# Transposed scores in the latent attention, a halved gate in the retention, and a new order of the first stage

## The chip, the cores and the metric

One Trainium2 chip, one of its cores. A core has five engines with queues of their own: TensorE (PE, matrix products into PSUM), VectorE (DVE), ScalarE (ACT), GpSimd (POOL) and SyncE (SP), which here issues the transfers. They meet through semaphores. The metric is the device time of one execution in microseconds (us).

## The reference

Six layers are applied to x (2 x 64 rows of 512), one after the other, each as x = x + layer(layernorm(x)): a latent cross-attention, an attention with sign-quantised weights, a mixture of 32 experts, a second cross-attention, a retention with group norm and gate, and a mixture of 128 mixed experts. The change touches the first and the fifth, and the sums of absolute weights of the second.

```
# first: latent cross-attention, 16 heads, 1024 context rows of 128
q_hk   = (layernorm(x) @ Wq.T).reshape(b, s, H, K)
q_big  = einsum('bshk,hkq->bshq', q_hk, w_kc_q)
kv     = kv_c * cos + rotate_half(kv_c) * sin           # rope
scores = einsum(q_big @ W_qr, kv @ W_kr)                # b h s l
ctx_c  = einsum('bhsl,bld->bhsd', softmax(scores), kv)
out    = einsum('bhsd,hkd->bshk', ctx_c, w_kc_kv).reshape(b, s, H*K) @ Wo.T
# fifth: retention
y   = ((q @ k.T) * 32**-0.5 * decay) @ v                # q, k rotated, 16 heads of 32
yn  = (y - mean) / sqrt(var + eps) * gn_weight + gn_bias
out = (silu(x @ w_g) * yn) @ w_proj
```

## The kernel before

All 128 rows of x stand on the 128 partitions. Each engine has one program, written out in order, and the order of the work is that of these programs.

**First stage.** The weights of the 16 heads come in four groups. SP issues, in this order: x, the constants (identity, mask and more), the query weights of group 0 in two halves, rank weights 0, wkr, query and rank weights 1, the same of 2, the context, the rope tables, query and rank weights 3, ctx64, then the 5 MB of wb. For a group g, `queries(g)` (L1077) makes the queries, `qrk_products(g)` (L1064) and `qkw_products(g)` (L1103) multiply the low-rank weights together, and `latent_queries(g)` (L1117) joins both; DVE's `at_copy`, `bw_copy` and `qk_copy` and ACT's copies bring each result from PSUM to SBUF. POOL makes the rotated half of rope (L405 to L411), DVE the other half and the sum (`rope`, L685); `context_transposes` (L1091) and ACT's `kvT_copy` turn the result. PE's order is L1179 to L1201.

**The loop of units.** A unit is two heads of one batch element, 128 rows; there are 16. Loop L1202 has in each pass the scores of unit i (`scores`, 128 rows on the partitions, 1024 keys in two PSUM banks), the result transpose of i-3, the context products of i-2 and the eight transposes of the probabilities of i-1. DVE takes the row maximum (L729) and ACT the exponential with the row sum (L480); both then copy half of the transposed probabilities (L736, L488); DVE scales the context by the reciprocal sum (L744). DVE also sums the absolute weights of the next layer (L763), and ACT takes their signs (L513). Behind it come `latent_values` and the output product (L1229).

**The retention.** PE makes projections 0 and 1 (q, k), the gate (`projection(3)`) and v (`projection(2)`), each eight instructions at L1508, then scores (L1533), y (L1541), the residual, and 18 products of ones (`keep_clock`, L1038) that compute nothing. DVE meanwhile makes weight x gate and bias x gate (L941 to L943), y x weight, the variance, its root on ACT, the division and the bias, in two halves of 256 columns (L951 to L966). PE transposes each half (`gated_transposes`) and multiplies by w_proj (L1563).

`link` makes DVE wait for its own last result.

## Time and profile before

| What | us |
|---|---|
| median of 3 runs (lowest, highest) | 358.01 (357.06, 358.23) |
| the profiled execution | 358.2 |
| its span, first to last instruction | 356.4 |
| PE busy | 346.5 (97%) |
| DVE, ACT, POOL busy | 146.4, 92.4, 39.3 |

The span is what the profile shows; 1.8 us of the time lie around it. PE's busy share counts every instruction from its start to its modelled end, so it says that PE is seldom without work, not that the work is all needed. The first stage runs from 8 to about 45.7 us, the loop of units to about 117, the retention from 281 to about 310.

### The profile page before, as it was taken

The numbers are of one execution on the slowest core, as the hardware profiler recorded it, in microseconds if no ns is written. First come the engines' busy times: TensorE is split into PE (matmuls) and PEld (weight loads), VectorE is DVE, ScalarE is ACT, GpSimd is POOL, SyncE is SP. The second block draws the span as 40 slices with busy tenths as digits, with TensorE's granted clock in tenths as the row PEclk, the third lists the DMA queues.
The fourth block names the chain that finished last, engine by engine and source line by source line (L and its number), as shares of the span: only waits on it lengthen the run. The fifth ranks groups of instructions, "written<-read, shape, count | busy, mean of one in ns | idle before, by whom it ended". The sixth has DMA issues, their size and how long they took to land.

```text
span 356.4 us, 5185 instructions
## 1 busy us (share of the span) xinstructions
PE 346.5 (97%) x2108; PEld 211.2 (59%) x2110; DVE 146.4 (41%) x318; ACT 92.4 (26%) x185; POOL 39.3 (11%) x77
## 2 busy tenths in 40 slices
PE   8898999999999999999999999999999999999997
PEld 6798677777778557555444443434366545554455
DVE  2118465777552134835213212321276245653131
ACT  1011344556543001423313121212112125030110
POOL 1006000000000002023000000000049300102110
PEclk9999999999999999999999999999999999999999
DMA  7999999920000700007598999899989910000000
GB/s 249 424 422 451 411 427 423 417 99 3 0 2 2 294 0 2 0 2 295 206 403 356 371 425 362 348 419 388 428 346 424 428 54 2 0 0 0 2 0 29
DMA packets 7800, 79.41 MB, mean 223 GB/s; under 512 B 993, under 2 KB 1761, under 8 KB 2913
## 3 DMA queue, kind: packets, MB, share of 16 engines
q1 hardware_dynamic: 7776, 79.09, 54.4%
q8 instruction: 17, 0.28, 0.3%
q14 instruction: 7, 0.05, 0.0%
HBM read 78.82 MB, written 0.26 MB: 222 GB/s over the span
## 4 chain that ended last, share of the span: by engine, by line
PE 85%; DMA 6%; DVE 3%; SPq 2%; ACT 1%; issue 1%; ACTq 0%
PE ps L1411 12%; PE ps L1577 10%; PE ps L1137 8%; PE ps L1160 8%; DMA ra<-in_wq 6%; PE ps L1439 5%; PE ps L1458 4%; PE ps L1229 4%; PE ps L1508 4%; PE ps L1149 4%; PE ps L1394 3%; PE ps L1450 2%; PE ps L1280 2%; PE ps L1372 2%; PE ps L1300 1%; PE ps L1598 1%
## 5 line engine op out<-in xcount | busy, mean ns | idle before, releaser
L1411 PE MATMUL ps<-rd,ra 128*64 128x384 f32 x256 | 44.4, 489 | 0.1
L1411 PEld LDWEIGHTS ps<-rd,ra 128*64 128x64 f32 x256 | 18.0, 137 | 26.5 <-issue 26.1
L1160 PEld LDWEIGHTS ps<-rd,ra 128*128 128x128 f32 x256 | 29.9, 192 | 4.4 <-issue 4.1
L1160 PE MATMUL ps<-rd,ra 128*128 128x128 f32 x256 | 31.3, 275 | 0.0
L1137 PE MATMUL ps<-rd 128*128 128x512 f32 x64 | 30.2, 594 | 0.0
L900 DVE SCALAR_TENSOR_TENSOR ra<-ra,ps 128x192 f32<-128x192 f32 x16 | 5.7, 354 | 59.3 <-ACT ra L584 59.3
L1577 PE MATMUL ps<-rd,xnT 128*128 128x512 f32 x64 | 28.0, 593 | 0.0
L480 ACT ACTIVATE ra<-ps,sv 128x1024 f32<-128x1024 f32 x16 | 17.8, 1116 | 35.0 <-DVE sv L729 35.0
L1038 PE MATMUL ps<-ones 128*128 128x256 bf16 x161 | 24.0, 296 | 1.0 <-POOL ones L390 1.0
L729 DVE TENSOR_REDUCE sv<-ps 128x1 f32<-128x1024 f32 x16 | 19.6, 1222 | 12.5 <-PE ps L1137 12.5
L584 ACT ACTIVATE ra<-ps 128x192 f32<-128x192 f32 x16 | 5.3, 331 | 65.9 <-PE ps L1411 65.9
L396 POOL TENSOR_SCALAR sv<-sv 128x1 f32<-128x1 f32 x6 | 1.5, 249 | 188.0 <-DVE sv L666 184.8
L1038 PEld LDWEIGHTS ps<-ones 128*128 128x128 bf16 x161 | 16.6, 107 | 7.2 <-issue 3.4
L1577 PEld LDWEIGHTS ps<-rd,xnT 128*128 128x128 f32 x64 | 11.9, 190 | 14.2 <-issue 14.2
L1439 PE MATMUL ps<-rd,ra 128*64 128x512 f32 x64 | 17.3, 618 | 0.0
L1087 PE MATMUL ps<-xnT,ra 128*128 128x128 f32 x128 | 15.3, 278 | 2.0 <-DMA ra<-in_wq 1.9
L1149 PE MATMUL ps<-cst,ra 128*128 128x128 f32 x128 | 16.6, 273 | 0.0
L1087 PEld LDWEIGHTS ps<-xnT,ra 128*128 128x128 f32 x128 | 14.6, 192 | 2.8 <-DMA ra<-in_wq 2.6
L1137 PEld LDWEIGHTS ps<-rd 128*128 128x128 f32 x64 | 10.9, 190 | 7.8 <-issue 7.6
L1149 PEld LDWEIGHTS ps<-cst,ra 128*128 128x128 f32 x128 | 14.5, 141 | 0.0
L1508 PE MATMUL ps<-rb,xnT 128*128 128x512 f32 x32 | 14.3, 593 | 0.0
L1229 PE MATMUL ps<-rb,ra 128*128 128x512 f32 x32 | 14.1, 595 | 0.0
(259 smaller groups left out, 487.4 us busy)
## 6 DMA issues: line engine op xcount, KB each, us to landing
rd<-in_ring SPq DMA_DIRECT2D x8, 2560.0 KB, 8.8
rd<-in_ring SPq DMA_DIRECT2D x8, 2048.0 KB, 8.5
rd<-in_f1gu SPq DMA_DIRECT2D x8, 1024.0 KB, 14.2
rb<-in_wb SPq DMA_DIRECT2D x1, 5120.0 KB, 34.9
ra<-in_e SPq DMA_DIRECT2D x2, 2560.0 KB, 17.1
rb<-in_b SPq DMA_DIRECT2D x1, 5120.0 KB, 21.2
ra<-in_wr SPq DMA_DIRECT2D x4, 1152.0 KB, 15.3
ra<-in_wq SPq DMA_DIRECT2D x3, 1024.0 KB, 14.8
```

Source lines behind the costliest of these rows:

```text
L480: act.activation(prob_x[u % 2].rearrange("p j l -> p (j l)"), ps[:, 2 * (u % 2):2 * (u % 2) + 2, :].rearrange("p a n -> p (a n)"), ACT.Exp ...
L729: dve.tensor_reduce(mx_x[:, u:u + 1], ps[:, 2 * (u % 2):2 * (u % 2) + 2, :].rearrange("p a n -> p (a n)"), AX.X, ALU.max, negate=True).the ...
L1038: pe.matmul(ps[:, bank, 0:256], idle[:, 0:P], idle, start=True, stop=True)
L1087: ins = pe.matmul(ps[:, g % 2, h * P:(h + 1) * P], wq_x(g)[:, h, c, :], xnT[:, c, :], start=(c == 0), stop=(c == C - 1))
L1137: ins = pe.matmul(ps[:, 2 * (u % 2) + half, :], rows, kvT[:, u % 2, half * 512:half * 512 + 512], start=True, stop=True)
L1149: ins = pe.transpose(ps[:, 4 + half, j * P:(j + 1) * P], prob_x[u % 2][:, 4 * half + j, :], ident)
L1160: ins = pe.matmul(ps[:, 6, 0:P], probT_x[u % 2][:, j, :], kvr[:, u % 2, j, :], start=(j == 0), stop=(j == J - 1))
L1229: ins = pe.matmul(ps[:, 4, :], latT[:, h, :], wo_x[:, h, :], start=(h == 0), stop=(h == H0 - 1))
L1411: ins = pe.matmul(ps[CAP * e:CAP * e + CAP, 2 + p % 2, 0:2 * I0].rearrange("p (g n) -> p g n", g=2), moe_xq[q % 2][:, c, CAP * e4:CAP * e4 ...
L1439: ins = pe.matmul(ps[CAP * e:CAP * e + CAP, 4 + odd, :], hT[:, 0, CAP * e:CAP * e + CAP], slot_main[p % SLOTS][:, e, :], start=first, stop ...
L1508: ins = pe.matmul(ps[:, t, :], xnT[:, c, :], w_ret[:, c, t, :], start=(c == 0), stop=(c == C - 1))
L1577: ins = pe.matmul(ps[:, bank, 0:n], xnT[:, c, :], w[:, c, lo:lo + n], start=(c == 0), stop=(c == C - 1))
```

## The change

**Latent attention.** The scores are made turned: eight products of 128 keys x 128 rows (`score_blocks`), so the keys stand on the partitions and the probabilities need no transpose. The maximum of a row is now across partitions: DVE takes for each partition the maximum over four blocks (`partial_max`, twice), PE transposes the two results, DVE takes the maximum of each row, PE turns it into a row on all partitions (`max_broadcast`), ACT copies it, DVE subtracts (here: adds the negative) into SBUF and ACT takes the exponential in place. The context has a column of ones appended (`kv1`), so the context products give the row sum as a 129th column. The scaling moves from DVE to ACT, and so do the absolute sums of the weights, with ACT's Abs.

**First stage.** SP's order, PE's order and the split of rope between POOL and DVE are new: query weights 0 and 1 come first, the rank weights 2 behind the context and rope, and all constants but the identity behind ctx64. On PE queries 0 and 1 lead, scores 0 come ahead of `qrk_products(3)`, and scores 1 ahead of `qkw_products(3)`.

**Retention.** The gate projection is cut in two halves of 256 columns. The second runs behind the y products, with its own Tanh behind the root; its half of y is normalised first and multiplied by the gate at the end. keep_clock there falls from 18 to 3.

```diff
-        kvr = rd[:, 13824:15872].rearrange("p (b j d) -> p b j d", b=B, j=J)
-        kvT = rd[:, 15872:17920].rearrange("p (b l) -> p b l", b=B)
-        qk_x = rd[:, 17920:19968].rearrange("p (b h s) -> p b h s", b=B, h=H0)
-        prob_x = [ra[:, 1024 * i:1024 * i + 1024].rearrange("p (j l) -> p j l", j=J) for i in range(2)]
-        probT_x = [ra[:, 2048 + 1024 * i:3072 + 1024 * i].rearrange("p (j r) -> p j r", j=J) for i in range(2)]
+        kv1 = rd[:, 13824:15888].rearrange("p (b j d) -> p b j d", b=B, j=J)
+        kvr = kv1[:, :, :, 0:P]
+        kvT = rd[:, 15888:17936].rearrange("p (b l) -> p b l", b=B)
+        qk_x = rd[:, 17936:19984].rearrange("p (b h s) -> p b h s", b=B, h=H0)
+        probT_x = [ra[:, 1024 * i:1024 * i + 1024].rearrange("p (j r) -> p j r", j=J) for i in range(3)]
+        abs_x = ra[:, 3072:4096]
+        part_mx = xn[:, P:3 * P]
+        max_bc = xn[:, 3 * P:4 * P]
...
-            sp.dma_start(cst[:, :], consts_d).then_inc(ld_const, 16)
+            sp.dma_start(cst[:, 0:P], consts_d[:, 0:P]).then_inc(ld_const, 16)
             for half in range(2):
                 sp.dma_start(ra[:, A_R + 1024 * half:A_R + 1024 * half + 1024],
                              wq_d[0][:, 1024 * half:1024 * half + 1024]).then_inc((ld_q[0], ld_q0b_e0)[half], 16)
+            query_weights(1)
             rank_weights(0)
+            rank_weights(1)
             sp.dma_start(rd[:, 11264:12288], wkr_d).then_inc(ld_kr, 16)
-            for g in range(1, 3):
-                query_weights(g)
-                rank_weights(g)
+            query_weights(2)
             sp.dma_start(rd[:, 0:2048], ctx_d).then_inc(ld_ctx, 16)
             sp.dma_start(rd[:, 2048:3072], rope_d).then_inc(ld_ctx, 16)
+            rank_weights(2)
             query_weights(3)
             rank_weights(3)
             sp.dma_start(ctx64[:, :], ctx64_d).then_inc(ld_c64, 16)
+            sp.dma_start(cst[:, P:K_N], consts_d[:, P:K_N]).then_inc(ld_c64, 16)
...
+            for half in range(2):
+                ins = pool.tensor_tensor(*rope_operands(1, half), ALU.mult)
+            ins.then_inc(rope_swap, 1)
             rstd_of(1)
...
+            for g in range(GROUPS - 1):
+                query_copy(g)
+            kvT_copy(0)
+            kvT_copy(1)
+            query_copy(GROUPS - 1)
...
+                act.wait_ge(sub_done, u + 1)
+                p = probT_x[u % 3].rearrange("p j r -> p (j r)")
+                act.activation(p, p, ACT.Exp).then_inc(exp_done, 1)
+            def ctx_scale(u):
+                act.wait_ge(rec_done, u + 1)
+                if u >= 1:
+                    act.wait_ge(cT_ps, u)
+                act.activation(xn[:, 0:P], ps[:, 6, 0:P], ACT.Copy, scale=rr_x[:, u:u + 1]).then_inc(ctx_sb, 1)
...
+            def weight_sums(k):
+                if k == 0:
+                    act.wait_ge(ld_q0b_e0, 2 * 16)
+                m, a0, a1 = we_parts[k]
+                act.activation(abs_x[:, 0:a1 - a0], we[:, a0:a1], ACT.Abs,
+                               accum_out=asum[:, k // 4, m:m + 1]).then_inc(quant_done, 1)
+            def weight_signs(k):
+                _, a0, a1 = we_parts[k]
+                act.wait_ge(quant_done, 2 * k + 1)
+                act.activation(we[:, a0:a1], we[:, a0:a1], ACT.Sign).then_inc(quant_done, 1)
+            def max_copy(u):
+                act.wait_ge(maxT_ps, 2 * u + 2)
+                if u:
+                    act.wait_ge(sub_done, u)
+                act.activation(max_bc, ps[:, 5, 0:P], ACT.Copy).then_inc(max_sb, 1)
+            for u in range(UNITS):
+                if u >= 1:
+                    exp_unit(u - 1)
+                if u >= 2:
+                    ctx_scale(u - 2)
+                max_copy(u)
+                if u == 0:
+                    kvT_copy(3)
+                if u >= 2:
+                    ctxT_copy(u - 2)
+                if 4 <= u < 16:
+                    (weight_sums, weight_signs)[u % 2](u // 2 - 2)
+            exp_unit(UNITS - 1)
...
+            def gate_tanh(half):
+                act.wait_ge(t_ps, 3 + 2 * half)
+                cols = slice(256 * half, 256 * half + 256)
+                act.activation(ret_th[:, cols], ps[:, 3, cols], ACT.Tanh, scale=half_rstd).then_inc(ret_th_done, 1)
...
+            at_copy(1)
             bw_copy(0)
             qk_copy(0)
-            at_copy(1)
             bw_copy(1)
+            dve.wait_ge(ld_ctx, 2 * 16)
+            for half in range(2):
+                ins = dve.tensor_tensor(*rope_operands(0, half), ALU.mult)
+            link(ins)
+            rope_cosines(0)
+            rope_sum(0)
+            qk_copy(1)
             at_copy(2)
-            qk_copy(1)
+            rope_cosines(1)
             bw_copy(2)
-            dve.wait_ge(ld_ctx, 2 * 16)
-            rope(0)
-            rope(1)
-            at_copy(3)
+            dve.wait_ge(rope_swap, 1)
+            rope_sum(1)
...
+            def partial_max(u, half):
+                dve.wait_ge(s_ps, 2 * u + half + 1)
+                dve.tensor_reduce(part_mx[:, P * half:P * half + P],
+                                  ps[:, 2 * (u % 2) + half, :].rearrange("p (j r) -> p r j", j=4), AX.X,
+                                  ALU.max).then_inc(max_done, 1)
             def row_max(u):
-                dve.wait_ge(s_ps, u + 1)
...
+                dve.wait_ge(maxT_ps, 2 * u + 1)
+                dve.tensor_reduce(mx_x[:, u:u + 1], ps[:, 4, 0:2 * P], AX.X, ALU.max, negate=True).then_inc(max_done, 1)
+            def subtract_max(u):
+                dve.wait_ge(max_sb, u + 1)
+                if u >= 3:
+                    dve.wait_ge(ctx_ps, u - 2)
+                dve.tensor_tensor(probT_x[u % 3], unit_scores(u), max_bc.unsqueeze(1).broadcast_to([P, J, P]),
+                                  ALU.add).then_inc(sub_done, 1)
+            def ctx_reciprocal(u):
                 dve.wait_ge(ctx_ps, u + 1)
-                if u >= 1:
...
+                dve.reciprocal(rr_x[:, u:u + 1], ps[:, 6, P:P + 1]).then_inc(rec_done, 1)
+            partial_max(0, 0)
+            partial_max(0, 1)
+            row_max(0)
+            at_copy(GROUPS - 1)
+            subtract_max(0)
+            partial_max(1, 0)
+            bw_copy(GROUPS - 1)
+            for u in range(1, UNITS):
+                partial_max(u, 1)
+                if u == 1:
                     qk_copy(GROUPS - 1)
                     dve.wait_ge(c64T_ps, 1)
                     dve.tensor_copy(ctx64T[:, :], ps[:, 7, 0:P]).then_inc(c64T_ready, 1)
-                if i >= 2:
...
+                if u >= 2:
+                    ctx_reciprocal(u - 2)
+                row_max(u)
+                if u + 1 < UNITS:
+                    partial_max(u + 1, 0)
+                subtract_max(u)
...
+            dve.wait_ge(y_ps, 1)
+            dve.tensor_tensor(yf[:, col_a], ps[:, 4, 0:256], ret_aw, ALU.mult).then_inc(yw_var_done, 1)
+            for half, heads in enumerate((head_a, head_b)):
                 dve.wait_ge(sq_sqrt_done, half + 1)
                 ins = dve.tensor_reduce(g_var[:, heads], ret_sq[:, heads, :], AX.X, ALU.add)
             link(ins)
             dve.tensor_scalar(g_var, g_var, 1.0 / 32, EPS, ALU.mult, ALU.add).then_inc(yw_var_done, 1)
+            link(dve.tensor_tensor(yf[:, col_b], ps[:, 5, 0:256], gnwb[:, 0, col_b], ALU.mult))
...
+            divide_heads(head_a)
+            dve.tensor_tensor(yf[:, col_a], yf[:, col_a], ret_ab, ALU.add).then_inc(ret_o_done, 1)
+            divide_heads(head_b)
+            link(dve.tensor_tensor(yf[:, col_b], yf[:, col_b], gnwb[:, 1, col_b], ALU.add))
+            dve.wait_ge(ret_th_done, 2)
+            link(dve.scalar_tensor_tensor(ret_ag[:, col_b], ret_th[:, col_b], 1.0, ps[:, 3, col_b], ALU.add, ALU.mult))
+            dve.scalar_tensor_tensor(yf[:, col_b], ret_ag[:, col_b], half_rstd, yf[:, col_b], ALU.mult,
+                                     ALU.mult).then_inc(ret_o_done, 1)
...
+                    if g == GROUPS - 1 and j == 1:
+                        max_broadcast(0)
...
+            def score_blocks(u, j0, j1):
+                if j0 == 0:
+                    pe.wait_ge(qk_sb, u // 4 + 1)
+                    if u < 2:
+                        pe.wait_ge(kvT_sb, 2 * u + 2)
+                        pe.wait_ge(q_sb, GROUPS)
+                        pe.wait_ge(at_sb, GROUPS - 1 + u)
+                    else:
+                        pe.wait_ge(sub_done, u - 1)
+                rows = qk_x[:, u % 2, 2 * (u // 2):2 * (u // 2) + 2, :].rearrange("p h s -> p (h s)")
+                for j in range(j0, j1):
+                    ins = pe.matmul(ps[:, 2 * (u % 2) + j // 4, P * (j % 4):P * (j % 4) + P],
+                                    kvT[:, u % 2, P * j:P * j + P], rows, start=True, stop=True)
+                    if j % 4 == 3:
+                        ins.then_inc(s_ps, 1)
+            def partial_max_transposes(u):
+                pe.wait_ge(max_done, 3 * u + 2)
                 if u < 2:
-                    pe.wait_ge(kvT_sb, 2 * u + 2)
-                    pe.wait_ge(q_sb, GROUPS)
-                    pe.wait_ge(at_sb, GROUPS)
-                if u >= 2:
-                    pe.wait_ge(exp_done, u - 1)
-                rows = qk_x[:, u % 2, 2 * (u // 2):2 * (u // 2) + 2, :].rearrange("p h s -> p (h s)")
+                    pe.wait_ge(bw_sb, GROUPS - 1 + u)
                 for half in range(2):
-                    ins = pe.matmul(ps[:, 2 * (u % 2) + half, :], rows, kvT[:, u % 2, half * 512:half * 512 + 512],
-                                    start=True, stop=True)
-                ins.then_inc(s_ps, 1)
-            def prob_transposes(u):
+                    ins = pe.transpose(ps[:, 4, P * half:P * half + P], part_mx[:, P * half:P * half + P], ident)
+                ins.then_inc(maxT_ps, 1)
+            def max_broadcast(u):
+                pe.wait_ge(max_done, 3 * u + 3)
+                if u:
+                    pe.wait_ge(max_sb, u)
+                pe.transpose(ps[:, 5, 0:P], mx_x[:, u:u + 1].broadcast_to([P, P]), ident).then_inc(maxT_ps, 1)
...
+                    ins = pe.matmul(ps[:, 6, 0:P + 1], probT_x[u % 3][:, j, :], kv1[:, u % 2, j, :],
+                                    start=(j == 0), stop=(j == J - 1))
...
+                pe.wait_ge(sub_done, UNITS - 1 + g // 2)
...
             queries(0)
+            queries(1)
             qrk_products(0)
-            keep_clock(3)
+            qrk_products(1)
             qkw_products(0)
-            queries(1)
+            keep_clock(6)
             latent_queries(0)
-            qrk_products(1)
+            qkw_products(1)
             queries(2)
-            qkw_products(1)
+            latent_queries(1)
             qrk_products(2)
-            latent_queries(1)
+            context_transposes(0)
             qkw_products(2)
+            context_transposes(1)
             queries(3)
-            context_transposes(0)
+            latent_queries(2)
+            score_blocks(0, 0, J)
+            context_transposes(2)
+            partial_max_transposes(0)
             qrk_products(3)
-            context_transposes(1)
-            latent_queries(2)
-            context_transposes(2)
             context_transposes(3)
-            for i in range(UNITS + 3):
...
+            score_blocks(1, 0, J)
+            qkw_products(3)
+            latent_queries(3)
+            pe.wait_ge(kvT_sb, GROUPS)
+            pe.wait_ge(ld_c64, 2 * 16)
+            pe.transpose(ps[:, 7, 0:P], ctx64[:, :], ident).then_inc(c64T_ps, 1)
+            context_products(0)
+            for u in range(1, UNITS):
+                if u + 1 < UNITS:
+                    score_blocks(u + 1, 0, 3)
+                partial_max_transposes(u)
+                if u + 1 < UNITS:
+                    score_blocks(u + 1, 3, 6)
+                max_broadcast(u)
+                if u + 1 < UNITS:
+                    score_blocks(u + 1, 6, J)
+                if u >= 2:
+                    result_transpose(u - 2)
+                    context_products(u - 1)
+            latent_values(0)
+            latent_values(1)
+            result_transpose(UNITS - 2)
+            context_products(UNITS - 1)
+            latent_values(2)
+            result_transpose(UNITS - 1)
...
+            def gate_projection(half):
+                cols = slice(256 * half, 256 * half + 256)
+                for c in range(C):
+                    ins = pe.matmul(ps[:, 3, cols], xnT[:, c, :], w_ret[:, c, 3, cols], start=(c == 0), stop=(c == C - 1))
+                ins.then_inc(t_ps, 1)
...
-            projection(3)
+            gate_projection(0)
...
+            gate_projection(1)
             residual(1, 4, True)
-            keep_clock(18, 2)
+            keep_clock(3, 2)
...
```

## Rows read from the trace of the kernel before

**Rows 1.** The page, the granted clock of PE in 40 slices of the span.
```profile
PEclk9999999999999999999999999999999999999999
```

**Rows 2.** Chain of waits (start us, us, what), end of the loop of units.
```profile
99.49 1.72 PE ps L1137 x4
101.21 0.11 PE ps L1169
101.32 1.79 PE ps L1160 x16
103.11 0.87 PE ps L1149 x8
103.98 1.73 PE ps L1137 x4
...
116.88 3.44 PE ps L1229 x8
```

**Rows 3.** Timeline (start us, us, engine, line, operation; idle before), first stage.
```profile
15.68 3.84 PE L1087 MATMUL ps<-xnT,ra 128*128 128x128 f32 x32 [0.97 <-DMA ra<-in_wq]
...
27.52 5.49 POOL L410 TENSOR_TENSOR rd<-rd 128x512 f32<-128x512 f32 x4 [22.28 <-DMA rd<-in_rope]
...
28.87 0.76 DVE L707 COPY rd<-ps 128x256 f32<-128x256 f32 x2 [0.65 <-PE ps L1123]
...
30.14 1.84 DVE L687 TENSOR_TENSOR rd<-rd 128x1024 f32<-128x1024 f32 x1
...
30.37 3.84 PE L1087 MATMUL ps<-xnT,ra 128*128 128x128 f32 x32 [0.89 <-DMA ra<-in_wq]
...
34.01 1.21 DVE L687 TENSOR_TENSOR rd<-rd 128x1024 f32<-128x1024 f32 x1
...
38.94 0.66 PE L1100 MATMUL ps<-cst,rd 128*128 128x128 f32 x4 [0.69 <-ACT rd L467]
```

**Rows 4.** Chain of waits, the retention stage.
```profile
291.06 3.43 PE ps L1508 x8
...
300.38 1.39 PE ps L1541 x32
...
304.87 0.45 PE ps L1552 x2
```

**Rows 5.** Groups by line and form (busy us, mean ns; idle before), whole span.
```profile
L480 ACT ACTIVATE ra<-ps,sv 128x1024 f32<-128x1024 f32 x16 | 17.8, 1116 | 35.0 <-DVE sv L729 35.0
...
L493 ACT ACTIVATE ra<-ps 128x128 f32<-128x128 f32 x16 | 4.4, 278 | 3.6 <-PE ps L1169 3.6
...
L1169 PE MATMUL ps<-cst,xn 128*128 128x128 f32 x16 | 4.4, 274 | 0.5 <-ACT ra L493 0.5
...
L513 ACT ACTIVATE ra<-ra 128x1024 f32<-128x1024 f32 x4 | 4.3, 1066 | 0.0
...
L830 DVE TENSOR_REDUCE att_st<-ps 128x8 f32<-128x512 f32 x6 | 4.1, 690 | 2.9 <-PE ps L1300 2.9
...
L480 ACT ACTIVATION_READ_ACCUMULATOR ra<-ps,sv 128x1 f32 x16 | 3.1, 193 | 0.0
...
L740 DVE RECIPROCAL sv<-sv 128x1 f32<-128x1 f32 x16 | 2.4, 153 | 0.0
...
L621 ACT ACT_TABLE_LOAD x1 | 1.3, 1283 | 0.0
...
L958 DVE TENSOR_REDUCE sv<-ra 128x8 f32<-128x256 f32 x2 | 0.8, 415 | 0.2 <-ACT ra L625 0.2
```

**Rows 6.** Views of L934 and L936: durations in ns, min/median/max.
```profile
L934 DVE SCALAR_TENSOR_TENSOR ra<-ps,sv,xpos x2: 750/750/751, 287.3 to 290.7; 128x512 f32<-128x512 f32 x2
...
L936 DVE SCALAR_TENSOR_TENSOR ra<-ps,sv,xpos x4: 475/476/477, 288.0 to 291.7; 128x256 f32<-128x256 f32 x4
```

**Rows 7.** Chain of waits, the first stage.
```profile
34.86 1.46 PE ps L1073 x24
...
45.74 0.43 PE ps L1137
```

170 lines of the change are left out of this document (45 added, 125 removed).

## The prediction, made before the run

> **What bounds the kernel now.** I read the page first: TensorE (PE) is busy 97% of the span, and the granted clock is at its upper level, 2.4 GHz, in every slice [rows 1]. So work taken off PE counts in full where PE is back to back, and nowhere else; the chain of waits says where that is. In the latent attention one unit is four pieces: scores 1.72, context products 1.79, eight transposes of the probabilities 0.87, one result transpose 0.11, together 4.49 us, and the score groups of neighbouring units are 4.49 us apart with no wait between [rows 2]. There PE alone sets the pace. In the first stage it is different: PE waits 0.97 us for the second group's query weights and 0.89 us for the fourth's, and 0.69 us for a ScalarE copy [rows 3]. The transfers pace it. In the retention stage the chain leaves PE from the end of the y products (300.38 + 1.39) to the first gated transposes at 304.87; keep_clock fills that time [rows 4].
>
> **The change, part A: the loop of units.** The scores come out with the keys on the partitions, so the eight probability transposes go. A unit on PE is then eight score products and eight context products at 1.79 per eight [rows 2] (the 129th column, which gives the row sum, adds under 2 ns a product by 1.79/8/128 a column), two transposes of partial maxima, one broadcast of the maximum and the result transpose at 0.11 each: 1.80 + 1.80 + 4 x 0.11 = 4.03 us, 0.46 less than 4.49.
>
> Is PE still last? VectorE (DVE) per unit: two partial maxima over 512 elements, 0.69 each as the reduce of that size; the maximum over 256, 0.42; the subtraction over 1024, 1.23 (two of 0.69, less one start of 0.15; the rope product of 1024 ran 1.21 undisturbed) [rows 3, 5]; a reciprocal, 0.15 [rows 5]. The subtraction of unit u-1 ends, partial maximum 0.69, PE's transposes and back about 0.45 (the reciprocal hides there), maximum 0.42, the next unit's first partial maximum 0.69, subtraction 1.23: about 3.5 us for a circle that may take 4.03. Beside it runs broadcast (0.27 until it is visible) and ScalarE's (ACT) copy of it, 0.28 [rows 5], ready when the subtraction is. ACT: exponential 1.12, three small reads at 0.28, and in twelve iterations a weight sum or sign of at most 1.07 + 0.19 [rows 5]: 3.2 us. The weight sums move from DVE to ACT and are free as long as this stays under 4.03. So both covers hold by 0.5 to 0.8 us, and PE stays last.
>
> No row shows the partial maximum's read: four elements that lie 512 bytes apart in PSUM. Nearest is the stride of 8 bytes at L936: 256 elements in 0.476, where L934 takes 0.750 for 512 packed ones, so 256 elements are worth 0.274, the packed rate [rows 6]. Bounds: 0.69 (full rate) and 1.22 (data part doubled). I take 0.69, the nearest row. The Trainium skill speaks against it: "SBUF — State Buffer", § Door 1: The DMA port swizzle, says that PSUM has lines of two fp32 values and that patterns that are not contiguous slow down (it names matmuls). The row at 8 bytes, where each read is on another line, does not agree; by that rule the time would be that of rival (1) below, 361.
>
> The first and last units have less cover. Unit 1's maximum waits behind the score blocks of unit 2, and those of unit 3 wait for its subtraction: 1.45 us of PE idle. The last unit has no score blocks to hide its circle; there the moved latent_values(0) and (1) do it. My schedule: unit 1's iteration 3.55, units 2 to 14 13 x 4.03 = 52.4, unit 15 with the tail (context products of 14, latent values 0 to 2, context products of 15) 7.7. Sum 63.65 us from the scores of unit 2 to the output product. Before, it is 116.88 - 45.74 = 71.14 [rows 2, 7]. Saving 7.5, of which 1.8 is the context product of unit 0, now done ahead: 5.7 net.
>
> **Part B: the first stage.** From 4.30 MB at 15.65 us (the second query weights land) to 10.33 MB at 30.33 (the fourth) [rows 3] (megabytes: the transfers' sizes added up in their order) the queue moves 0.41 MB a us. In the new order that gives: query weights 1 at 11.1, rank weights 0 and 1 at 13.9 and 16.8, rope 24.5, rank weights 2 at 27.4, query weights 3 at 29.9. Moved back are the constants other than the identity, to behind ctx64 (the mask copy follows to unit 3, where DVE has slack), and rank weights 2, to behind ctx and rope. The 5 MB of wb and what follows it keep their place, since as many bytes stand ahead; the transfers that wait for semaphores shift with the work.
>
> PE then: queries 0 and 1 (3.6 each, 3.84 with the last one's latency [rows 3]) to 15.5 without the 0.97 wait, qrk 0 and 1 (1.46 each [rows 7]) to 18.5, qkw 0, latent queries 0 (after a DVE copy), qkw 1 and queries 2 to 25.15, latent queries 1 to 26.1. Here the wait comes back: qrk 2 needs rank weights 2, 27.4 to 28.9. Next are the context transposes 0, which need rope. DVE now does half of the swap itself: 24.5 + 2 x 0.69 + 1.21 + 1.23 = 28.3 undisturbed; but GpSimd multiplies at the same time, and where they overlapped the same DVE instruction took 1.84 instead of 1.21 [rows 3]. I add 1.2: 29.5. Behind it on DVE are qk_copy(1), 0.76 [rows 3], and at_copy(2), 0.42 as 256 elements, for which qkw 2 waits; then context transposes 1; queries 3 start at 31.7, though their weights are there at 29.9 (before: 30.37 [rows 3]). Bounds of this: 30.6 (no contention) to 32.3.
>
> After queries 3 (35.3): latent queries 2 to 36.2, scores 0 to 38.0, context transposes 2, a wait of 0.35 for the partial maximum, its transposes, qrk 3 with the broadcast in the middle, context transposes 3 to 41.1, a wait of 0.8 for kvT_copy(3), scores 1 to 43.7, qkw 3, 0.8 for bw_copy(3), latent queries 3 to 46.15, 0.8 for qk_copy(3), context products 0 to 48.75. Queued behind each wait is all of PE. Scores of unit 2 start at 48.75 instead of 45.74: 3.0 later, 1.8 of it the context product above. Left: 1.2 lost. Attention in all: 7.5 - 3.0 = 4.5; I take 4.4.
>
> **Part C: retention.** The gate projection's second half (half of 3.44 by its eight instructions of 0.43 [rows 4], so 1.72) goes behind the y products, where keep_clock ran. PE is not 1.72 but 1.36 earlier at projection(2), since the transposes of k wait 0.37 for the rotation. From there all shifts by 1.36 (v copies, the Sqrt table load of 1.28 [rows 5], scores, y). In the DVE chain the second square no longer waits for the second product (0.2 less); half b is multiplied by weight and bias instead, beside the root. The first gated transposes start at about 303.3 instead of 304.87. The second half has two instructions more (0.42 + 0.48) and waits for the second Tanh, whose table load (1.28 as the Sqrt one) runs 301.9 to 303.15 beside that DVE chain; the half is ready at 305.1, where PE wants it at 305.1. The products with w_proj move with it: 1.6 saved. Cover gone: if Tanh is 0.6 late, 0.6 is lost. The other table load ahead of the router's exponential goes; it was hidden.
>
> **Sum.** The profiled execution took 358.2 us (span 356.4), the median of the runs is 358.01, 0.2 off; both stand for the same time. 358.2 - 4.4 - 1.6 = 352.2.
>
> **The rivals.** (1) Slower: the strided partial maximum costs double, 1.22. The DVE circle is 3.5 + 1.06 = 4.6, DVE sets the pace; 13 units lose 0.56, the first and last the full 1.06: +9, so 361. It decides from the point where one partial maximum takes about 1.1 (15 units x the excess over the slack eat 6.0). For: 512 bytes is far from the 8 measured. Against: the row at 8 bytes shows nothing at all. 6%. (2) The first stage loses more: rope at its late bound, or the context products and score groups a little late in each hand-over, 2 us in all: 354.3. For: seven waits of PE in a row, each on an estimated copy. 15%. (3) The change does not do what it says: Abs is not in ACT's loaded table, and each of six weight sums brings two loads of 1.28 [rows 5] before the next exponential; ACT 5.8 per such unit, 6 x 1.7 = +10: 362. Against: Sign runs among the exponentials without one. 2%. The Trainium skill, "ScalarE: Activation LUTs", § Table sets: the hidden batching unit, has abs in every set; no run here shows it yet. (4) PE's clock falls to 1.2 GHz in the first stage, whose longest PE idle grows from 0.97 to 1.45; a fall of 5 us costs 2.5: 354.7. 3%. (5) DMA and rope are at their early bound, hand-overs short: 350.6. 13%.
>
> **How the numbers follow.** Forecast 352.2 (350.9 to 353.5): 56%. Five in 100 stay for a wait that I have not seen, four of them within 0.3% and one slower. The range 349.8 to 356.0 holds the forecast, (2), (4) and (5), and leaves out (1), (3) and those five: 13%. 0.3%, 1.1 us, is about what a measurement of this kernel tells from no change. Faster by more: 56 + 15 + 3 + 13 = 87%; within: 4%; slower: 6 + 2 + 1 = 9%.
>
> **What would show it.** Score groups of neighbouring units 4.03 apart with no idle on PE; partial maximum 0.69; subtraction 1.23; no table load among the units. Scores of unit 2 at 48.75, output product near 112.4. Queries 3 at 31.7, released by DVE and not by a DMA. First gated transposes 1.6 earlier relative to the stage's start. A partial maximum of over 1 us, or PE idle on the subtraction in each unit, makes the prediction wrong; so does a first stage that reaches unit 2 after 51.

## The result, and the profile after

The changed kernel takes 356.07 us (median of 7 runs, 354.72 to 356.83); the kernel before, measured beside it, 358.01 (7 runs, 357.06 to 359.18). The ratio is 0.9940, interval 0.9923 to 0.9956: 1.9 us faster, which is clear of the noise, and far from the 6.0 us forecast. The profiled execution took 356.3 us, its span is 354.5.

The page of the kernel after: busy time of each engine, then the granted clock in 40 slices, then the new groups of the loop of units (busy us, mean ns, idle before).

```profile
PE 339.9 (96%) x2216; PEld 221.1 (62%) x2218; DVE 153.6 (43%) x332; ACT 97.2 (27%) x198; POOL 37.0 (10%) x76
...
PEclk9998999999999999999999999999999999999999
...
L1203 PE MATMUL ps<-rd 128*128 128x128 f32 x256 | 36.0, 276 | 2.0 <-DVE ra L784 1.3
...
L772 DVE TENSOR_REDUCE xn<-ps 128x128 f32<-128x512 f32 x32 | 21.8, 681 | 1.5 <-PE ps L1203 1.5
...
L784 DVE TENSOR_TENSOR ra<-ps,xn 128x1024 f32<-128x1024 f32 x16 | 19.6, 1224 | 2.5 <-ACT xn L524 0.7
```

The two numbers that decided over the loop are as forecast: the strided partial maximum takes 681 ns, the subtraction 1224. The first row also says where the gain went: TensorE's busy time fell by 6.6 us (from 346.5), the span by only 1.9, so 4.7 us of new waiting stand on TensorE. What is new, too, is the 8 in the clock's fourth slice, where [rows 1] has a 9 throughout.

The chain of waits after (start us, us, what; a line on DVE in it means that PE had to wait for that), from the rope sum to the scores of unit 3, and the end of the loop:

```profile
28.50 1.23 DVE rd L726
...
30.77 1.06 PE ps L1178 x8
31.83 1.04 PE ps L1163 x4
32.88 4.36 PE ps L1150 x32
37.24 0.89 PE ps L1188 x8
38.13 2.03 PE ps L1203 x16
...
50.11 2.02 PE ps L1229 x16
52.14 0.67 PE ps L1203 x6
...
55.58 0.91 PE ps L1203 x6
...
106.23 0.17 PE ps L1220
...
108.75 0.33 PE ps L1213 x2
...
116.52 4.72 PE ps L1305 x11
```

Read it against [rows 2]. The output product starts at 116.52; before it started at 116.88. So attention as a whole, meant to gain 4.4, gained 0.4. The loop did its part: from the scores of unit 2 (52.1 here, 51.97 in the timeline) to the output product it takes 64.5 us instead of 71.1. But it starts at 51.97 instead of 45.74, where the forecast said 48.75. The loss lies ahead of the loop.

Retention, the same view:

```profile
283.37 6.90 PE ps L1584 x16
...
300.10 1.92 PE ps L1590 x8
...
307.86 0.71 DVE sv L700
```

The second half of the gate projection (L1590, 300.10) lies behind the y products, and the stage takes 283.37 to 307.86, 24.49 us; before it was 283.74 to 309.74, 26.00. That is 1.5 of the 1.6 forecast. (The first gated transposes, L1635 at 303.21, came 1.3 earlier relative to the start of the stage, where the forecast had 1.6; the last pair came 1.5 earlier.)

### The profile page after: what moved, and what is told of

The parts are those of the page before. It is cut to its first block, busy times and chain, and to the rows that moved or that the text cites. A ratio compares the mean times of both kernels' runs of the same rounds, so it can differ in the third digit from the quotient of the medians.

```text
span 354.5 us, 5415 instructions
## 1 busy us (share of the span) xinstructions
PE 339.9 (96%) x2216; PEld 221.1 (62%) x2218; DVE 153.6 (43%) x332; ACT 97.2 (27%) x198; POOL 37.0 (10%) x76
## 4 chain that ended last, share of the span: by engine, by line
PE 85%; DVE 6%; DMA 5%; SPq 2%; issue 1%; ACT 1%
PE ps L1487 12%; PE ps L1660 10%; PE ps L1229 8%; PE ps L1203 8%; DMA rd<-in_rope 5%; PE ps L1515 5%; PE ps L1534 4%; PE ps L1305 4%; PE ps L1470 3%; PE ps L1584 3%; PE ps L1526 2%; PE ps L1356 2%; PE ps L1448 2%; PE ps L1376 1%; PE ps L1681 1%; PE ps L1150 1%
## 5 line engine op out<-in xcount | busy, mean ns | idle before, releaser
L1203 PE MATMUL ps<-rd 128*128 128x128 f32 x256 | 36.0, 276 | 2.0 <-DVE ra L784 1.3
L1203 PEld LDWEIGHTS ps<-rd 128*128 128x128 f32 x256 | 32.7, 194 | 2.5 <-issue 2.5
L1229 PE MATMUL ps<-rd,ra 128*128 128x129 f32 x256 | 31.3, 275 | 0.8 <-DVE rd L743 0.8
L772 DVE TENSOR_REDUCE xn<-ps 128x128 f32<-128x512 f32 x32 | 21.8, 681 | 1.5 <-PE ps L1203 1.5
L1099 PE MATMUL ps<-ones 128*128 128x256 bf16 x149 | 21.4, 285 | 1.0 <-POOL ones L399 1.0
L784 DVE TENSOR_TENSOR ra<-ps,xn 128x1024 f32<-128x1024 f32 x16 | 19.6, 1224 | 2.5 <-ACT xn L524 0.7
L1099 PEld LDWEIGHTS ps<-ones 128*128 128x128 bf16 x149 | 14.8, 103 | 6.4 <-issue 3.2
L490 ACT ACTIVATE ra<-ra 128x1024 f32<-128x1024 f32 x16 | 16.8, 1052 | 4.0 <-DVE ra L784 3.8
L1470 PE MATMUL ps<-ra 128*128 128x256 bf16 x96 | 12.9, 273 | 0.6 <-issue 0.6
L548 ACT ACTIVATE xnT<-ps 128x256 f32<-128x256 f32 x5 | 1.9, 384 | 41.8 <-PE ps L1116 41.8
## 6 DMA issues: line engine op xcount, KB each, us to landing
rb<-in_wb SPq DMA_DIRECT2D x1, 5120.0 KB, 31.7
```

The source lines that it names most:

```text
L490: act.activation(p, p, ACT.Exp).then_inc(exp_done, 1)
L772: dve.tensor_reduce(part_mx[:, P * half:P * half + P], ps[:, 2 * (u % 2) + half, :].rearrange("p (j r) -> p r j", j=4), AX.X, ALU.max).the ...
L784: dve.tensor_tensor(probT_x[u % 3], unit_scores(u), max_bc.unsqueeze(1).broadcast_to([P, J, P]), ALU.add).then_inc(sub_done, 1)
L1099: pe.matmul(ps[:, bank, 0:256], idle[:, 0:P], idle, start=True, stop=True)
L1203: ins = pe.matmul(ps[:, 2 * (u % 2) + j // 4, P * (j % 4):P * (j % 4) + P], kvT[:, u % 2, P * j:P * j + P], rows, start=True, stop=True)
L1229: ins = pe.matmul(ps[:, 6, 0:P + 1], probT_x[u % 3][:, j, :], kv1[:, u % 2, j, :], start=(j == 0), stop=(j == J - 1))
```

## The experiments

The theory after the result: the new loop and the new retention are worth what was said, and the new first stage gives back what they bring, in three ways: rope late, the clock, and short hand-overs in a row. The rival: the loop itself is worth less, because DVE or the extra latency of a unit sets its pace. A second rival: the stage is paced by transfers, so that its order on PE changes nothing. "DMA" below is the transfers that SP's queue issues. Times are medians; "scores of unit 3" and "output product" are starts in the profiled execution. The kernel before was run again beside each group of experiments and gave 357.79 (e1 to e4), 358.05 (e5 to e8) and 358.28 (e9 to e11); ratios are to these, and a difference under 0.5 us between two groups means nothing.

**e1_ret_only: the retention part alone, on the kernel before.** The edit, on PE (DVE and ACT follow in halves):

```diff
-            projection(3)
+            gate_projection(0)
...
+            gate_projection(1)
             residual(1, 4, True)
-            keep_clock(18, 2)
+            keep_clock(3, 2)
```

> The kernel before with the retention part of the change alone. In the trace of the changed kernel the retention, from projection(0) to the statistics of the next norm, took 24.5 us instead of 26.0. If the parts are independent (theory), this kernel is 1.5 us faster than before, 356.5. Rival: the gain is in the trace of one run only, or the earlier end of the stage is given back while the next stage's weights land; then under 0.5 us.

Measured: 355.96 (355.59 to 356.76), ratio 0.9946 [0.9923, 0.9969], 1.8 us; the stage runs from 283.01 to 307.50, again 24.49. So retention alone gives as much as the whole change does, and attention in the changed kernel gives about nothing.

**e2_clock: idle products in the two longest waits of the first stage of the changed kernel.**

```diff
             latent_queries(1)
+            keep_clock(8, 3)
             qrk_products(2)
+            keep_clock(12, 3)
             context_transposes(0)
```

> The changed kernel, with 8 products of ones before qrk_products(2) and 12 before context_transposes(0), where PE idled 0.9 and 1.4 us. Theory: these two waits and a third of 0.3 us let PE's clock fall to 1.2 GHz from 31.0 to 34.8 us; with them filled the clock stays at its upper level in the whole first stage, queries(3) takes 3.8 instead of 4.6 us, and the output product starts 1.5 to 1.9 us earlier (116.5 to about 114.8). Rival: the fall has nothing to do with these waits, or the time it costs is given back by the next wait; then the output product stays within 0.5 us of 116.5.

Measured: 355.08 (354.88 to 355.77), ratio 0.9920 [0.9891, 0.9949], 1.0 less than the changed kernel. The rows that belong to it are these. The windows of the changed kernel (stretch, its length, PE busy and instructions, granted clock, DMA share, GB/s):

```profile
28.00:31.00 3.00, 1.31 (x18) 1.00 1.06 432
31.00:32.00 1.00, 1.00 (x9) 0.50 1.31 540
32.00:33.00 1.00, 1.00 (x6) 0.50 1.32 563
33.00:34.00 1.00, 1.00 (x7) 0.50 0.76 328
34.00:35.00 1.00, 1.00 (x9) 0.80 0.95 410
```

and the timeline of the filled kernel at the last group's query products:

```profile
32.40 3.74 PE L1150 MATMUL ps<-xnT,ra 128*128 128x128 f32 x32
```

In the changed kernel PE works 1.31 of the 3 us from 28 to 31, and then the clock stands at 0.50, its level of 1.2 GHz, for about 3.4 us: the eight products at L1178 take 1.06 instead of 0.66, the four transposes behind them 1.04 instead of 0.66, the 32 query products 4.36 instead of 3.57 (the second of each pair is from the next experiment). Together 1.57 us. Filled, no slice is below 1.00, and the output product starts at 115.42 instead of 116.52: 1.1 earlier, where I had expected 1.5 to 1.9, but the rope data had landed 0.5 later. In four of the seven runs of the changed kernel the mean clock is 1.000 and in three 0.995; their medians are 355.3 and 356.4. So the fall costs 1.1 to 1.6 us in the executions that have it. Between medians it explains a quarter of the shortfall (1.0 of 3.9 us), not all: even the four runs without it are 3.1 us over the forecast.

No fall in the four runs of e2 against three in seven proves little by itself. Counted over all runs that have a clock on record, a mean clock of 0.995 or less stands in 9 of 27 with the new first stage and its long waits (the changed kernel, e8, e9), in 1 of 12 where these waits were filled or shortened (e2, e3, e7), and in 3 of 64 with the old first stage or nearly that (the kernel before, e1, e4 to e6, e10, e11). So the fall belongs for the most part to the waits that the new order brought; it is not theirs alone.

**e3_rope: GpSimd starts its rope product only when DVE's half is done.**

```diff
             pool.wait_ge(ld_ctx, 2 * 16)
+            pool.wait_ge(rope_ready, 1)
             for half in range(2):
                 ins = pool.tensor_tensor(*rope_operands(1, half), ALU.mult)
```

> The changed kernel, with GpSimd's rope product held back until DVE has finished rope(0). Theory: the two engines slow each other; DVE's swap falls from 2.25 to 1.4 us, its cosine product from 2.06 to 1.21, and rope(0) is ready at 28.1 instead of 29.7. Context transposes(0) then follow qrk_products(2) with no wait, PE's clock does not fall, and the output product starts 2.5 to 3.4 us earlier, about 113.5. Rival: rope(1) is then late (GpSimd ends at about 30.5) and DVE's later copies wait for it; gain under 1 us.

Measured: 353.82 (353.56 to 355.69), ratio 0.9896 [0.9857, 0.9935]; output product at 114.10, 2.4 earlier, although the rope data landed 0.9 later here. The timeline of DVE and GpSimd, first the changed kernel:

```profile
24.11 2.25 DVE L755 TENSOR_TENSOR rd<-rd 128x512 f32<-128x512 f32 x2 [2.00 <-DMA rd<-in_rope]
26.40 2.06 DVE L722 TENSOR_TENSOR rd<-rd 128x1024 f32<-128x1024 f32 x1
28.50 1.23 DVE L726 TENSOR_TENSOR rd<-rd 128x1024 f32<-128x1024 f32 x1
...
24.22 3.16 POOL L416 TENSOR_TENSOR rd<-rd 128x512 f32<-128x512 f32 x2 [18.77 <-DMA rd<-in_rope]
```

then this one (its lines are one further down):

```profile
24.97 1.29 DVE L756 TENSOR_TENSOR rd<-rd 128x512 f32<-128x512 f32 x2 [1.97 <-DMA rd<-in_rope]
26.29 1.22 DVE L723 TENSOR_TENSOR rd<-rd 128x1024 f32<-128x1024 f32 x1
27.55 1.23 DVE L727 TENSOR_TENSOR rd<-rd 128x1024 f32<-128x1024 f32 x1
...
28.95 3.25 POOL L417 TENSOR_TENSOR rd<-rd 128x512 f32<-128x512 f32 x2 [23.49 <-DVE rd L727]
```

One wait on an engine that has nothing else to do makes DVE's swap 1.29 instead of 2.25 and its cosine product 1.22 instead of 2.06. Rope is ready 3.8 us after its data instead of 5.6 and PE finds it there. In this execution the clock stays up; one of the other three runs, the slowest (355.69), has a mean clock of 0.995. The two engines' products delay each other, and the one that nobody waits for yet should go second: behind, it meets one DVE product only, which takes 1.48 instead of 1.21. The prediction had this contention, at 1.2 us; it is 1.8.

**e4_old_first: the first stage of the kernel before, with the new loop and retention.** The last part of PE's order there (the transfers, rope and the rest of PE's order are as before too; DVE's order around units 0 and 1 was fitted to it):

```diff
...
+            qkw_products(2)
+            queries(3)
             context_transposes(0)
-            qkw_products(2)
+            qrk_products(3)
             context_transposes(1)
-            queries(3)
             latent_queries(2)
+            context_transposes(2)
+            context_transposes(3)
             score_blocks(0, 0, J)
-            context_transposes(2)
+            qkw_products(GROUPS - 1)
+            score_blocks(1, 0, 3)
             partial_max_transposes(0)
-            qrk_products(3)
-            context_transposes(3)
-            score_blocks(1, 0, J)
-            qkw_products(3)
-            latent_queries(3)
+            score_blocks(1, 3, 6)
+            max_broadcast(0)
+            score_blocks(1, 6, J)
+            latent_queries(GROUPS - 1)
...
```

> The changed kernel with the transfers, PE's order and rope of the first stage as they were before; the new loop of units and the retention stay. It undoes the first-stage part. Theory (the new first stage is a loss): scores(0) start at 39.6 as before instead of 38.1, but unit 2's scores at about 49 instead of 52.1, the output product at 113.5 instead of 116.5, the time about 353.2. Rival (the new first stage is a gain, and the forecast gain went in the loop): output product later than 116.5, time above 356.

Measured: 353.39 (352.58 to 354.70), ratio 0.9871 [0.9832, 0.9909]; scores of unit 3 at 53.04 instead of 55.58, output product at 113.97. So the new first stage as a whole (transfers, order and rope together; no run takes these apart) makes the kernel 2.7 us slower, the fall of the clock included. e4 and e3, the new first stage with the rope wait (353.82), are level within the spread.

**e5_loop_only: the same, with the retention of before.** The edit is e4's without that of e1.

> The loop of the changed kernel alone: first stage and retention as in the kernel before. With the earlier variants the parts would add up: the old first stage with new loop and new retention ran in 353.4, and the retention part alone was worth 1.8. Theory (loop worth 4.4 us, the new first stage costs about 2.7): 355.2, between 354.7 and 355.8, output product about 114.0 as with the old first stage. Rival (the parts do not add, the retention part is worth less behind the new loop): 354.3 or less. If the loop were worth the 5.7 us of the prediction: 352.3.

Measured: 354.95 (354.33 to 357.64), ratio 0.9918 [0.9900, 0.9935]. The parts add: the ratios of e5 (loop) and e1 (retention) multiply to 0.9864, and e4, which has both, has 0.9871. The new loop with the context products of unit 0 ahead of it is worth 3.1 us, then, and not the 5.7 of the prediction's part A, which would have given 352.3 here. Its profiled execution is its slowest run, and shows why. Windows, with the same columns as above:

```profile
30.00:32.00 2.00, 0.26 (x2) 1.00 1.19 494
32.00:34.00 2.00, 2.00 (x14) 0.64 1.02 439
34.00:36.00 2.00, 2.00 (x11) 0.51 1.28 555
```

and the row of the timeline that belongs to them:

```profile
31.74 5.46 PE L1121 MATMUL ps<-xnT,ra 128*128 128x128 f32 x32 [2.06 <-DMA ra<-in_wq]
```

The last group's query weights landed at 31.7 here, at 30.3 in e4 by the same order of transfers; the wait of 2.06 us was followed by the clock's fall, and the products took 5.46 instead of 3.84.

**e6_old_c0: e4, and the context products of unit 0 no longer ahead of the loop.**

```diff
             pe.transpose(ps[:, 7, 0:P], ctx64[:, :], ident).then_inc(c64T_ps, 1)
-            context_products(0)
...
                 if u >= 2:
                     result_transpose(u - 2)
-                    context_products(u - 1)
+                context_products(u - 1)
```

> The old first stage with the new loop and retention, but the context products of unit 0 no longer ahead of the loop: they follow the scores of unit 2. Theory: with unit 0's context products first, TensorE waits 1.5 us for the copy of the last latent queries and 1.3 us for unit 1's subtraction; with the scores of unit 2 in their place the wait for the copy goes (those scores need the queries of group 0 alone) and the 1.8 us of context products lie over the circle of unit 1. The start of unit 3's scores moves from 53.0 to about 51.1, the output product from 114.0 to about 112.1, the time from 353.4 to about 351.5. Rival (the circle of unit 1 on VectorE, not the order on TensorE, sets the start of unit 3's scores): nothing gained, 353.4. It decides for the rival if unit 3's scores still wait over 1 us for the subtraction.

Measured: **350.47** (349.18 to 351.13), ratio 0.9793 [0.9764, 0.9823]. It is faster than both kernels, by 7.6 and by 5.6 us. Chain of e4, then of this kernel:

```profile
46.76 0.67 DVE rd L738 x2
...
47.57 2.02 PE ps L1214 x16
49.59 0.67 PE ps L1188 x6
...
51.67 1.24 DVE ra L777
52.90 0.14 issue
53.04 0.91 PE ps L1188 x6
```

```profile
45.38 0.91 PE ps L1188 x6
...
47.85 1.79 PE ps L1214 x16
49.64 0.67 PE ps L1188 x6
```

In e4 PE stops for the last copy of the latent queries (DVE L738), which only the context products' bank needs, and again for unit 1's subtraction (L777). With the scores of unit 2 (L1188) first, which don't need that copy, the 1.79 us of context products (L1214) lie over unit 1's circle on DVE, and the scores of unit 3 start at 49.64 instead of 53.04. Output product: 110.33 instead of 113.97.

Not all of these 3.4 and 3.6 us are the edit's. The first scores already start at 38.94 here and at 39.87 in e4, 0.9 earlier, though nothing ahead of them was edited: the transfers landed earlier, and a wait of 0.50 for rope didn't come. What is left, 2.5 us at the scores of unit 3 and 2.7 at the output product, is the two waits of e4 (1.53 and 1.27) less the 0.27 that remains in front of the scores of unit 2. I had expected 1.9; the medians differ by 2.9.

**e7_rope_c0: both edits, e3's and e6's, on the changed kernel.**

> The changed kernel with two edits: GpSimd's rope product behind VectorE's first half (as in the run before, 353.8), and the context products of unit 0 behind the scores of unit 2. Theory (both losses lie in the hand-overs, independent of which first stage is used): the 0.8 us wait for the last copy and the 1.3 us for unit 1's subtraction go, unit 3's scores start at about 51.2 instead of 53.2, the output product at about 112.1, time 351.8. Then the new first stage would be level with the old one once both are free of these waits. Rival (the new first stage stays worse): over 352.5.

Measured: 351.46 (350.73 to 351.66), ratio 0.9817 [0.9799, 0.9836], 2.4 less than e3; output product at 111.84. The edit of e6 is worth about the same on this first stage. Free of its two faults, the new first stage stands 1.0 us behind the old one (e6), with intervals that overlap: that it is worse is not shown, and nothing speaks for its being better.

**e8_q3_first: the last group's query products ahead of the first context transposes, on the changed kernel.**

```diff
             qrk_products(2)
+            queries(3)
             context_transposes(0)
             qkw_products(2)
             context_transposes(1)
-            queries(3)
```

> The changed kernel with one move on TensorE: the last group's query products ahead of the first context transposes, which need the rope result. Theory (the placing of a product that waits for rope in front of 3.6 us of work that does not is what costs the first stage, and the fall of the clock follows from that wait): no wait over 0.9 us between 28 and 36, granted clock at 1.00 throughout, first scores at about 36.6 instead of 38.1, output product about 115.0 instead of 116.5, time 354.6. Rival A (the transfers pace it: the last group's query weights land as late as the rope result is ready): first scores at 38, time 356. Rival B (the fall of the clock comes from the waits before 29 and happens all the same): the query products still take 4.6 us, time 356.

Measured: 356.01 (355.06 to 359.42), ratio 0.9955 [0.9926, 0.9983]: nothing gained. Timeline:

```profile
27.23 1.53 PE L1136 MATMUL ps<-ra 128*64 128x128 f32 x24 [0.97 <-DMA ra<-in_wr]
30.77 3.84 PE L1150 MATMUL ps<-xnT,ra 128*128 128x128 f32 x32 [2.00 <-DMA ra<-in_wq]
```

My theory fell here, rival A holds: with rope out of the way PE waits 2.00 us for the query weights instead, and what it could have done in that time now stands behind them. First scores at 37.76, against 38.13. The clock stayed at 1.00 in this execution, behind waits of 0.97 and 2.00, longer than those behind which it fell in the changed kernel (0.90 and 1.41); in three of the ten runs it did fall. So one long wait goes with the fall in some executions and not in others, and what else decides is open.

**e9_dve_extra: the second partial maximum done twice in units 2 to 14, on the changed kernel.**

```diff
+                if 2 <= u < UNITS - 1:
+                    dve.wait_ge(s_ps, 2 * u + 2)
+                    link(dve.tensor_reduce(part_mx[:, P:2 * P],
+                         ps[:, 2 * (u % 2) + 1, :].rearrange("p (j r) -> p r j", j=4), AX.X, ALU.max))
                 partial_max(u, 1)
```

> The changed kernel with one partial maximum (128x512, 0.68 us) done twice on VectorE in each of the units 2 to 14: 13 times 0.68 = 8.9 us of VectorE work more, nothing else. Theory (TensorE paces a unit, and VectorE has about 0.6 us to spare in front of the transposes of the partial maxima: it ends that maximum at 84.15 and the transposes start at 84.83): a unit grows by 0.05 to 0.15 us, the output product comes 0.6 to 2 us later, time 356.7 to 358. Rival (VectorE is already the pace of the loop, and 4.07 instead of 4.03 a unit is its doing): all 8.9 us are added, 365. The slack of the prediction (circle of 3.5 in 4.03) gives 0.16 a unit, 2.1 in all: 358.2.

Measured: 357.98 (357.44 to 359.55), ratio to the kernel before 0.9995 [0.9978, 1.0012], 1.9 above the changed kernel for 8.9 us more on DVE. In its timeline context products of neighbouring units start at 80.23 and 84.46 (L1233), 4.23 apart; after the change it was 4.07. The 0.16 a unit is what the prediction's slack gives (3.5 + 0.69 against 4.03). The rival, DVE as the pace of the loop, is refuted: cover of 0.5 us a unit is really there. (The profiled execution took 359.35: its clock fell as in the changed kernel, behind waits of 0.85 and 1.43, and the last query products took 5.01; the loop behind that is not touched.)

**e10_q1_first and e11_fill: two tries to better e6.** In e10 the idea that names the change, alone:

```diff
+            query_weights(1)
             rank_weights(0)
...
             queries(0)
+            queries(1)
             qrk_products(0)
             keep_clock(3)
             qkw_products(0)
-            queries(1)
```

and in e11 seven idle products (`keep_clock(7, 3)`) ahead of `queries(3)`.

> The best kernel so far (old first stage, new loop with the context products of unit 0 behind the scores of unit 2, new retention: 350.5) with the idea that gives the change its name alone: the query weights of group 1 are transferred ahead of the first rank weights, and the query products of two groups come first. Theory (the transfers pace the first stage: the last group's query weights land near 30.1 in any order, since the same bytes are ahead of them): the wait for group 1's weights (0.8) goes, and comes back in front of the last group's query products, which still start near 30.2; scores of unit 2 at 45.4, time 350.5, the same within 0.3%, or 0.5 to 1 slower in executions in which the clock falls after that longer wait. Rival (TensorE's work sets the stage): 0.8 us gained, 349.7.

> The same best kernel with seven idle bfloat16 products (about 0.8 us) in front of the last group's query products, where TensorE waits 0.5 to 2 us for their weights. Theory (after a long wait there the granted clock falls in some executions, which costs 1 to 1.6 us when the 32 products take 4.6 to 5.5 us instead of 3.84): with the wait filled the products take 3.84, no slice of the first stage shows a clock under 1.00, and the slowest executions come down; median 350.3, the highest under 351. Rival (the fill only delays the products where the weights are early): 350.8.

Measured: 351.06 (350.16 to 351.51) and 351.17 (350.20 to 351.96), ratios 0.9782 [0.9761, 0.9803] and 0.9787 [0.9767, 0.9808]; e6 has 0.9793. No two of the three can be told apart. e11 missed what I expected (350.3, the highest under 351). The timeline of e10, then of e11:

```profile
30.76 3.84 PE L1138 MATMUL ps<-xnT,ra 128*128 128x128 f32 x32 [0.78 <-DMA ra<-in_wq]
```

```profile
30.29 0.94 PE L1088 MATMUL ps<-ones 128*128 128x256 bf16 x7
31.87 3.84 PE L1137 MATMUL ps<-xnT,ra 128*128 128x128 f32 x32 [0.64 <-DMA ra<-in_wq]
```

Transferring the query weights first brings nothing: the last group's weights land near 30 to 32 in whatever order the earlier ones come. With the fill the clock stayed up in this execution, although those weights landed as late as in e5's slowest one (3.84 instead of 5.46); that the fill did it, one execution can't show. Its median and its highest run are no lower than e6's, where the mean clock is 0.999 or more in all four. As insurance it costs at most 0.7 us; that it gains is not shown.

## Why the prediction was wrong

Its sign was right; retention was right and the loop nearly so, and the first stage was wrong. By its own steps:

- **What bounds the kernel**: right. TensorE is 96% busy, units 2 to 14 have no wait in them, and e9 shows that DVE's 8.9 us more cost 1.9.
- **Strided partial maximum**: right, 681 ns against 0.69, and rival (1) is refuted. The rule on two-value lines of PSUM ("SBUF — State Buffer", § Door 1: The DMA port swizzle, in the Trainium skill) does not show in this DVE read at a stride of 512 bytes.
- **Unit on PE**: 4.03 forecast, 4.07 to 4.09 measured. The chain gives the piece: the broadcast of the maximum (L1220) takes 0.17 where I had 0.11 by the transpose's row. Thirteen units: 0.8 us. Unit 1 (3.61 for 3.55) and the last unit with the tail (7.77 for 7.7) were right. The loop took 64.55 from the scores of unit 2 instead of 63.65.
- **Abs on ACT**: right. The trace has no table load among the units, rival (3) is refuted; the rule cited for it ("ScalarE: Activation LUTs", § Table sets: the hidden batching unit, in the Trainium skill) agrees.
- **Retention**: right, 1.5 in the trace and 1.8 alone in e1, for 1.6.
- **First stage**: here the prediction failed (part B, the schedule from rope to the context products of unit 0). The scores of unit 2 start at 51.97 instead of 48.75, 3.2 us late, over my own limit of 51. Three terms make it. (a) The clock, which I priced at 2.5 us with a chance of 3% and left out of the sum: 1.57 us in this execution. (b) Rope: ready at 29.72 for my 29.5, which is near by luck. I had the contention right in kind and too small by 0.6 (I took twice the 0.63 that L687 lost in [rows 3]; the product behind it in the same trace, L690, took 2.07 instead of 1.23), and data that landed 0.4 earlier hid most of it. The last query products started at 32.88 for my 31.7, 0.8 of it by the clock; the first scores are 1.93 late, 1.57 of it the clock and 0.4 this. (c) The hand-overs from the first scores to the context products of unit 0: 11.98 us instead of 10.75. The waits were forecast well (0.35, 0.8, 0.8, 0.8 and 1.45; the trace has 0.35, 0.73, 0.79, 0.83 and 1.27). What I left out is that a group of products behind or ahead of a wait shows its latency (the time until its last result is there): 2.02 for sixteen score products instead of 1.79, 1.17 for the latent queries instead of 0.89, 0.44 for two transposes instead of 0.22, and two halves of 0.81 for qrk 3 instead of 1.46.

With the clock (1.6), the rest of rope (0.4), the latencies (1.2) and the loop (0.9), the 4.1 us between 352.2 and the profiled 356.3 are accounted for. Rival (2), "the first stage loses 2 us more", named the right place and its mechanism, and rival (4) the other one; I gave them 15% and 3% as if only one could come. In the profiled execution both did, and the counts under e2 say that the fall mostly comes with such waits. The range had room for either alone. The runs without a fall have a median of 355.3, 3.1 over the forecast: 0.9 of that is the loop, and the rest is about the 2 us of (2).

There is an error under these, in the question I asked. I compared the new first stage with the old one under the old loop (1.2 net lost) and never asked what the old one would do under the new loop. e4 answers: it would be 2.7 us better. Nor does part A's 5.7 hold with the old first stage: e5 gives 3.1. The loop is 0.9 longer than forecast, and the context products of unit 0, counted at 1.8, also bring a wait of 1.5 for the last copy. The waits of 0.8 and 1.45 stood in my own schedule, both caused by these products going first; moving them by one pass is worth 2.4 to 2.9 us (e6, e7). That a stage whose weights pace it (e8, e10) gains nothing from a new order of products could be read from [rows 3]: 0.41 MB a microsecond puts the last query weights near 30 in either order.

## What to carry to other kernels

When a change reorders a stage that transfers pace, work out first when its last input lands: reordering can't win before that time, and every product that it puts in front of a late helper result can lose. Price a short wait of TensorE with the latency of the group behind it (0.2 us here) and add the clock's fall to each rival that makes the engine idle, since the two often come together (9 of 27 runs here). And when a schedule written for the prediction shows a wait, ask at once which independent work could stand in it; here moving one group of products was worth more than the whole change.

## What the runs showed of the hardware

Two products with both operands in SBUF, one on DVE and one on GpSimd, slow each other. For the changed kernel, then for e3 (durations in ns, lowest, median and highest; then first and last start in us):

```profile
L755 DVE TENSOR_TENSOR rd<-rd x2: 693/1170/1647, 24.1 to 24.7; 128x512 f32<-128x512 f32 x2
L416 POOL TENSOR_TENSOR rd<-rd x2: 1597/1598/1598, 24.2 to 25.8; 128x512 f32<-128x512 f32 x2
```

```profile
L756 DVE TENSOR_TENSOR rd<-rd x2: 682/686/691, 25.0 to 25.6; 128x512 f32<-128x512 f32 x2
L417 POOL TENSOR_TENSOR rd<-rd x2: 1156/1647/2138, 28.9 to 30.1; 128x512 f32<-128x512 f32 x2
```

Alone, half a swap takes DVE 0.69 us and GpSimd 1.16. In the changed kernel DVE's first half is as fast as alone, its second takes 1.65 and the cosine product 2.06 instead of 1.22, 1.8 lost in all; GpSimd's two take 1.60 each, 0.9 lost. In e3 GpSimd's first product is undisturbed (1.16), its second, beside DVE's cosine product, takes 2.14. The Trainium skill, "SBUF — State Buffer", § SBUF: two separate sides, says of this pair (a DVE instruction with two SBUF inputs against a GpSimd operation that reads SBUF) that whichever starts first has their shared ports for a whole instruction while the other is blocked fully. The trace agrees, if the two take turns: GpSimd's first product ends 1.0 behind DVE's first half (24.80), DVE's second half 0.5 behind that (25.82), GpSimd's second 1.0 behind that (26.36), the cosine product 1.1 behind that (27.38), each its own time alone less about 0.15. So the price of such an overlap here is what remains of the other engine's instruction, once for each turn, and not a fixed factor.

The same weights behind the same transfers were waited for until times between 29.9 us (e1) and 31.7 (e5) in different executions, as much as most edits here are worth. And the granted clock fell to 1.2 GHz behind waits of 1.41, 1.43 and 2.06 us (the changed kernel, e9, e5) and stayed at 2.4 GHz behind waits of 1.31 and 2.00 (e1, e8); what else decides it, no run here shows.
